# A cross-network tower on one Trainium2 core: product (2, 6) of layer 2 split like its neighbours, its difference on VectorE

## The chip, the cores and the metric

The kernel runs on one core of a Trainium2 chip. The metric is the device time of one execution in microseconds. The engines are TensorE (PE in the profile; its weight loads are PEld), VectorE (DVE), ScalarE (ACT), GpSimd (POOL) and SyncE (SP), whose queue issues most DMAs.

## The reference

The batch has 1024 rows. 32 tables are looked up with `ids`, giving `x0` of 32 fields by 16 embedding elements for each row. Three cross layers follow:

```python
for i in range(n_layers):
    z = (x0[:, :, None, :] * h[:, None, :, :]).reshape(B, F * G, E)
    y = jax.nn.relu(jnp.einsum('oc,bce->boe', Ws[i], z) + bs[i][None, :, None])
    if i != n_layers - 1:
        half = y.shape[1] // 2
        x_keep, h = (y[:, :half, :], y[:, half:, :])
    else:
        x_keep, h = (y, y)
    xs.append(x_keep)
return jnp.sum(jnp.concatenate(xs, axis=1), axis=2)
```

Each layer has 128 outputs; layers 1 and 2 have 32 x 64 = 2048 inputs, the products of a field with a row of the layer before. The sums over the embedding, joined with 16 dense features, go through three dense layers (272 to 512, to 256, to 1). All values are float32.

## The kernel before, in words

The work is cut into 32 tiles of 128 batch rows by 4 embedding elements, 512 columns each; four tiles make a block of 128 rows. An *item* (layer, n) is two chunks of 128 products (128 x 1024 values). VectorE multiplies (L1070), TensorE sums the products with the weights (L617, L625, L640) into one PSUM bank per layer, ScalarE adds the bias, applies the relu and hands `h` to the next layer (`go_on`, L815; `keep`, L821).

There are two kinds of item. A **whole** item is a plain fp32 product: VectorE writes it to one of four `prod` buffers, TensorE takes it with two fp32 matmuls (L617), which the trace shows as four records. A **split** item is written to `unsplit`; ScalarE casts it to fp32r in `high` (L829); `low` = unsplit - high is made by a subtraction whose inputs and output are all in SBUF (`split_low`: L500 on GpSimd, L1078 on VectorE). TensorE then takes four matmuls of `high`, with the high and low parts of the weights (L625), and two of `low` (L640). `kind_of` (L99) says which kind an item is: layers 0 and 1 are whole, layer 2 is split with its difference on GpSimd, except (2, 6), which is whole with weights of its own, `w2T_whole`. In the last slot (2, 2), (2, 5) and (2, 7) have their difference on VectorE.

The order is written out by hand. In steady state all engines go through the same list of 19 steps per tile, a *slot*:

```python
SLOT = [(1, 0), (1, 1), (2, 0), (1, 2), (2, 1), (1, 3), (0, 0), (2, 2), TAIL, (1, 4), (0, 1),
        (2, 3), (1, 5), (2, 4), (1, 6), (2, 5), (1, 7), (2, 6), (2, 7)]
```

Layer 1 belongs to the slot's tile, layer 0 to the tile after, layer 2 to the tile before. TAIL is half an item of layer 0, split between ScalarE (L852, L853) and GpSimd (`tail_parts`, L508). TensorE takes the `low` of a split item one item later (`multiply_low` in `slot`). It transposes the next tile's fields after (2, 4) (`turn_x`, L589), and ScalarE copies them out after (2, 5) (`take_x`, L809). After (2, 4) ScalarE waits for (0, 1) and makes h0 (`next_h0`). After (1, 1) VectorE adds to `acc_kept` (L1101, or L1097 for the first tile of a block).

GpSimd issues the 32 table lookups of the block after next in its slots (L490), eight a slot, placed by `LOOKUPS_FIRST` and `LOOKUPS_AFTER` behind its differences:

```python
LOOKUPS_AFTER = ((0, 0, 2, 0, 1, 2, 3), (0, 0, 1, 1, 1, 2, 2))
LOOKUPS_FIRST = (0, 1)
```

The first row is for *quarter* 0, the second for quarters 1, 2 and 3. A slot has quarter 0 if in it a new block begins for the lookups: after (2, 2) ScalarE waits for the block's 32 lookups to land and copies them to `emb` (`take_rows`, L793), then goes on to TAIL; GpSimd takes the next ids after that (`begin`) and looks up again. Per quarter 0, with layer-2 items 0 to 5 and 7, GpSimd issues two lookups after (2, 2), one after (2, 4), two after (2, 5) and three after (2, 7); in the other quarters one first, one after each of (2, 2), (2, 3), (2, 4), two after (2, 5) and two after (2, 7).

Of the kernel before, what the change touches and what calls it, by code (L numbers as in the profile page):

```python
# [38 lines left out]
P = 128  # L39
# [6 lines left out]
ITEM = 2  # L46
GROUP = 4
CHUNKS = FIELDS * HALF // P
GROUPS = CHUNKS // GROUP
# [36 lines left out]
WHOLE, BY_POOL, BY_DVE = range(3)  # L86
SPLIT = (BY_POOL, BY_DVE)
RING = (4, 4, 2)
WHOLE2 = (2, 6)
LAST_BY_DVE = [(2, 2), (2, 5), (2, 7)]  # L90

ADD_KEPT_AFTER = (1, 1)
# [5 lines left out]

def kind_of(item, last):  # L99

    if item[0] < 2 or item == WHOLE2:
        return WHOLE
    return BY_DVE if last and item in LAST_BY_DVE else BY_POOL

# [18 lines left out]
def of_kind(items, kind, last=False):  # L125
    return [x for x in items if x != TAIL and kind_of(x, last) == kind]


class Plan:
# [13 lines left out]
    def kind(self, s, item):  # L143
        return kind_of(item, self.is_last(s))
# [22 lines left out]
def dlrm_tower(nc, dense_ctx, ids, tables, w_top1, b_top1, w_top2, b_top2, w_top3,  # L167
# [8 lines left out]
    with ExitStack() as ctx:  # L176
        def sb(name, shape, dt=F32):
            return ctx.enter_context(nc.sbuf_tensor(name, shape, dt))
# [20 lines left out]
        w0T = sb("w0T", [P, GROUP, P])  # L199
        w0T_tail = sb("w0T_tail", [P, P], F32R)  # L200
        w1T = sb("w1T", [P, CHUNKS, P])
        w2T_high = sb("w2T_high", [P, CHUNKS, P], F32R)
        w2T_low = sb("w2T_low", [P, CHUNKS, P], F32R)
        w2T_whole = sb("w2T_whole", [P, ITEM, P])
        wt3 = sb("wt3", [P, TOP2 // P])

        dense_parts = sb("dense_parts", [P, batch], F32R)
# [347 lines left out]
        def _(pe):  # L555
# [20 lines left out]
            for b in range(BLOCKS):  # L576
                last = pe.transpose((y0, y1)[b // GROUP][:, P * (b % GROUP):P * (b % GROUP + 1)], dense_wide[:, b, :],
                                    ident[:, :])
# [14 lines left out]
            def accumulator(s, layer):  # L593
                return y2[(s[1] - 1) % 2] if layer == 2 else (y0, y1)[layer]

            def begin_layer(s, layer):

                if layer == 0:
                    pe.wait_ge(s_kept0, number(s) + 1)
                elif layer == 1:  # L600
                    pe.wait_ge(s_kept1, number(s))
                elif not isinstance(s[0], int) or number(s) >= 2:
                    pe.wait_ge(s_sum2, number(s) - 2 + 1)

            def multiply(s, item):

                layer, n = item
                y = accumulator(s, layer)
                if n == 0:
                    begin_layer(s, layer)  # L610
                e, kind = plan.entry(s, item), plan.kind(s, item)
                if kind == WHOLE:
                    z = prod[plan.place(s, item, RING)]
                    pe.wait_ge(s_made[kind], e + 1)
                    for c in range(ITEM):
                        w = w2T_whole[:, c, :] if layer == 2 else (w0T, w1T)[layer][:, ITEM * n + c, :]
                        last = pe.matmul(y[:, :], w, z[:, c, :], start=(n == 0 and c == 0),  # L617
                                         stop=(item in (LAST0, LAST1) and c == ITEM - 1))
                    last.then_inc(s_used[kind], 1)
                else:  # L620
                    z = high[kind][plan.place(s, item, RING)]
                    pe.wait_ge(s_high[kind], e + 1)
                    for c in range(ITEM):
                        for w in (w2T_high, w2T_low):
                            pe.matmul(y[:, :], w[:, ITEM * n + c, :], z[:, c, :],  # L625
                                      start=(n == 0 and c == 0 and w is w2T_high), stop=False)
# [17 lines left out]
            def slot(s, between={}):  # L644
                items = plan.items(s)
                nxt = after(s, 2)
                turn_after = (2, 4) if (2, 4) in items else items[-1]
                waiting = None
                for item in items:
                    if item != TAIL:  # L650
                        multiply(s, item)

                    if waiting:
                        multiply_low(s, waiting)
                    waiting = item if item == TAIL or plan.kind(s, item) != WHOLE else None
                    if item in between:
                        first_unit(between[item])
                    if item == turn_after and (not isinstance(s[0], int) or number(nxt) < TILES):
                        if waiting and item == items[-1]:
                            multiply_low(s, waiting)  # L660
                            waiting = None
                        turn_x(nxt)
                if waiting:
                    multiply_low(s, waiting)
# [4 lines left out]
            for n, c in enumerate(FIRST_ORDER):  # L669
                pe.wait_ge(s_rotated, n + 1)  # L670
                for e in range(QUAD):
                    last = pe.transpose(first_shifted[c][:, P * e:P * (e + 1)], rotated[c][:, P * e:P * (e + 1)], ident[:, :])
# [12 lines left out]
            def top1(unit, col):  # L685

                _, n, m = unit
                rows = slice(TOP1 * n, TOP1 * (n + 1))
                cols = slice(TOP1 * col + P * m, TOP1 * col + P * (m + 1))
                return three_passes(unit_bank[unit][:, :], wt1_high[:, cols], wt1_low[:, cols],  # L690
                                    z_high[n][col][:, :], z_low[col][:, rows], stop=(col == 1))
# [249 lines left out]
        def _(dve):  # L941
# [40 lines left out]
            for n, home in enumerate(homes):  # L982
                dve.wait_ge(s_turned, n + 1)
                source = prep[1][:, 0, :] if n == 1 else prep[n % 2]
                if n == 1:
                    dve.tensor_copy(home, source).then_inc(s_tail_w, 1)

                    dve.wait_ge(s_tail_w, 1)
                    for quarter in (1, 3):
                        lanes = slice(FIELDS * quarter, FIELDS * (quarter + 1))  # L990
                        last = dve.tensor_tensor(w0T_tail[lanes, :], source[lanes, :],
                                                 w0T_tail[lanes, :].bitcast(F32), ALU.subtract)
                    last.then_inc(s_stored, 1)
                elif n in lows:
                    if WHOLE2[1] // (GROUP // ITEM) == n - 2 - GROUPS:
                        of = ITEM * WHOLE2[1] % GROUP
                        dve.tensor_copy(w2T_whole[:, :, :], source[:, of:of + ITEM, :])
                    dve.tensor_copy(home, source).then_inc(s_w_high, 1)

                    dve.wait_ge(s_w_high, sorted(lows).index(n) + 1)  # L1000
                    dve.tensor_tensor(lows[n], source, home.bitcast(F32), ALU.subtract).then_inc(s_stored, 1)
                else:
                    dve.tensor_copy(home, source).then_inc(s_stored, 1)
# [229 lines left out]
```

## Time and profile before

| | |
|---|---|
| median of 3 runs | 1061.19 us (1061.14 to 1063.73) |
| the profiled execution, its own time | 1066.62 us |
| its span | 1064.8 us |
| TensorE busy | 995.8 us (94%) |
| VectorE busy | 821.8 us (77%) |
| ScalarE busy | 474.4 us (45%) |
| GpSimd busy | 816.3 us (77%) |
| mean granted TensorE clock | 0.976 of full speed |

The profile comes from one execution; the span runs from its first to its last instruction. The times in the rows are microseconds from the span's start, with mean durations in nanoseconds in the tables by tile. Busy times count each engine's own instructions. Records of TensorE are pipelined and overlap, so the pace is read from the starts of successive records, not from their durations.

### The profile page before, as it was taken

Reading aid. Unit: us, or ns where it says so; the run is one execution under the profiler, and the core shown is the slowest. Engines: PE = TensorE matmul, PEld = TensorE weight load, DVE = VectorE, ACT = ScalarE, POOL = GpSimd, SP = SyncE. Lnnn points to the kernel's source line nnn. Section 1 sums busy time; section 2 is a strip of 40 time slices with the busy share of each in tenths; the row PEclk is TensorE's granted clock in tenths of the full one; section 3 lists DMA queues with packets and bytes.
Section 4 is the critical chain, followed back from the end, with each engine's and each line's share of the span. In section 5 each row is a group of like instructions: output and inputs, shape, how many; then the busy total and the mean of one; then the engine's idle time right before and its main releaser. Section 6 shows DMA issues by size and latency. Waiting matters only on the chain.

```text
span 1064.8 us, 11324 instructions
## 1 busy us (share of the span) xinstructions
PE 995.8 (94%) x3089; PEld 572.8 (54%) x3089; DVE 821.8 (77%) x750; ACT 474.4 (45%) x595; POOL 816.3 (77%) x524
## 2 busy tenths in 40 slices
PE   3178899999999999999999999999899999999988
PEld 2133455555555555555555555555455555555565
DVE  6234877798778977899778977898778977788882
ACT  2222544444544454454444454444444454543443
POOL 7655779887998879887998789886998766566540
PEclk9579999999999999999999999999999999999989
DMA  8089999989888888899888888888888888889000
GB/s 158 10 189 198 205 199 190 210 191 197 191 194 191 191 192 185 192 198 208 191 194 186 194 188 190 187 192 191 195 187 188 192 186 192 190 186 219 30 1 0
DMA packets 49012, 185.45 MB, mean 174 GB/s; under 512 B 17570, under 2 KB 22178, under 8 KB 28388
## 3 DMA queue, kind: packets, MB, share of 16 engines
q1 hardware_dynamic: 40804, 183.15, 78.2%
q0 software_dynamic: 8192, 2.11, 2.0%
q8 instruction: 7, 0.11, 0.0%
q14 instruction: 9, 0.07, 0.0%
HBM read 182.06 MB, written 3.15 MB: 174 GB/s over the span
## 4 chain that ended last, share of the span: by engine, by line
POOL 42%; PE 26%; issue 18%; DMA 7%; DVE 4%; ACT 2%; SPq 0%; POOLq 0%; ACTq 0%; DVEq 0%
POOL low L500 24%; POOL looked_up L490 16%; PE y L617 15%; PE y L625 6%; DMA looked_up<-in_tbl,ids_now 4%; PE y L640 3%; POOL tail_parts L508 2%; DMA spread<-xcols 2%; DVE unsplit L1070 1%; DVE prod L1070 1%; DMA xcols<-xrows 0%; ACT emb L793 0%; ACT tail_high L853 0%; PE y L721 0%; DVE acc_kept L1101 0%
## 5 line engine op out<-in xcount | busy, mean ns | idle before, releaser
L500 POOL TENSOR_TENSOR low<-unsplit,high 128x1024 fp32r<-128x1024 f32 x221 | 525.1, 2388 | 113.3 <-ACT high L829 111.5
L617 PE MATMUL y<-prod,w1T 128*128 128x512 f32 x1024 | 480.3, 597 | 5.4 <-ACT kept L821 2.7
L1070 DVE TENSOR_TENSOR prod<-spread,h 128x1024 f32<-128x1024 f32 x288 | 349.1, 1216 | 118.3 <-PE y L617 102.6
L829 ACT CAST high<-unsplit 128x1024 fp32r<-128x1024 f32 x224 | 234.0, 1045 | 243.6 <-DVE unsplit L1070 243.2
L1070 DVE TENSOR_TENSOR unsplit<-spread,h 128x1024 f32<-128x1024 f32 x224 | 272.1, 1215 | 48.8 <-ACT h L815 48.6
L490 POOL DMA_INDIRECT looked_up<-in_tbl,ids_now x256 | 248.7, 971 | 69.1 <-issue 59.4
L617 PEld LDWEIGHTS y<-prod,w1T 128*128 128x128 f32 x1024 | 193.5, 192 | 166.8 <-issue 144.1
L625 PE MATMUL y<-high,w2T_high 128*128 128x512 f32 x448 | 226.7, 506 | 4.4 <-ACT high L829 4.4
L640 PE MATMUL y<-low,w2T_high 128*128 128x512 f32 x448 | 202.7, 533 | 6.3 <-POOL low L500 6.3
L625 PE MATMUL y<-high,w2T_low 128*128 128x512 f32 x448 | 177.9, 397 | 0.0
L815 ACT ACTIVATE h<-y,bias 64x512 f32<-64x512 f32 x128 | 83.3, 651 | 209.2 <-PE y L617 208.3
L640 PEld LDWEIGHTS y<-low,w2T_high 128*128 128x128 f32 x448 | 84.4, 191 | 91.3 <-issue 61.5
L617 PE MATMUL y<-prod,w0T 128*128 128x512 f32 x256 | 122.2, 600 | 5.5 <-DVE prod L1070 5.5
L625 PEld LDWEIGHTS y<-high,w2T_high 128*128 128x128 f32 x448 | 84.9, 190 | 50.0 <-issue 29.4
L625 PEld LDWEIGHTS y<-high,w2T_low 128*128 128x128 f32 x448 | 84.9, 190 | 43.4 <-issue 29.0
L1070 DVE TENSOR_TENSOR prod<-shifted,xT 128x1024 f32<-128x1024 f32 x64 | 77.7, 1215 | 22.8 <-DMA shifted<-xcols 15.4
L617 PEld LDWEIGHTS y<-prod,w0T 128*128 128x128 f32 x256 | 48.9, 192 | 49.3 <-issue 45.0
L508 POOL TENSOR_TENSOR tail_parts<-tail,tail_high 128x512 fp32r<-128x512 f32 x32 | 41.0, 1283 | 25.7 <-ACT tail_high L853 25.6
L617 PE MATMUL y<-prod,w2T_whole 128*128 128x512 f32 x128 | 60.1, 592 | 0.0
L821 ACT ACTIVATE kept<-y,bias_kept 64x512 f32<-64x512 f32 x64 | 43.7, 682 | 1.6
L809 ACT COPY xrows<-xT 48x512 f32<-48x512 f32 x32 | 18.5, 579 | 50.6 <-PE xT L589 50.6
L589 PE MATMUL xT<-ident,four_times 128*128 128x128 f32 x128 | 20.2, 282 | 22.2 <-ACT four_times L801 22.2
(115 smaller groups left out, 441.3 us busy)
## 6 DMA issues: line engine op xcount, KB each, us to landing
spread<-xcols SPq DMA_DIRECT2D x128, 1024.0 KB, 9.0
shifted<-xcols SPq DMA_DIRECT2D x124, 256.0 KB
shifted_tail<-xcols SPq DMA_DIRECT2D x124, 64.0 KB
looked_up<-in_tbl,ids_now POOLq DMA_INDIRECT x256
xcols<-xrows SPq DMA_DIRECT2D x32, 96.0 KB, 2.0
spread<-in_L_rec_W SPq DMA_DIRECT2D x3, 512.0 KB, 7.0
spread<-in_L_rec_W SPq DMA_DIRECT2D x1, 1024.0 KB, 11.6
wt<-in_W_top SPq DMA_DIRECT2D x2, 512.0 KB, 8.7
```

What stands on the lines that cost most here:

```text
L490: pool.indirect_dma_start(out=looked_up[:, f, :], out_offset=None, in_=tables[f][:, :], in_offset=bass.IndirectOffsetOnAxis(ap=ids_now[:, ...
L500: pool.tensor_tensor(low[kind][r][:, :, :], unsplit[kind][r][:, :, :], high[kind][r][:, :, :].bitcast(F32), ALU.subtract).then_inc(s_low[k ...
L508: pool.tensor_tensor(tail_parts[:, :], tail[:, :], tail_high[:, :].bitcast(F32), ALU.subtract).then_inc(s_tail_low, 1)
L589: last = pe.transpose(xT[:, P * e:P * (e + 1)], four_times[:, e, :, :].rearrange("p a f -> p (a f)"), ident[:, :])
L617: last = pe.matmul(y[:, :], w, z[:, c, :], start=(n == 0 and c == 0), stop=(item in (LAST0, LAST1) and c == ITEM - 1))
L625: pe.matmul(y[:, :], w[:, ITEM * n + c, :], z[:, c, :], start=(n == 0 and c == 0 and w is w2T_high), stop=False)
L640: last = pe.matmul(accumulator(s, layer)[:, :], w2T_high[:, ITEM * n + c, :], z[:, c, :], start=False, stop=(item == LAST2 and c == ITEM - 1))
L809: act.copy(xrows[:, :], xT[0:XROWS, :]).then_inc(s_xrows, 1)
L815: last = act.activation(h[to, :], y[lanes, :], ACT.Relu, bias=bias[lanes, :])
L821: act.activation(kept[t[1] % KEPT][lanes, :], y[lanes, :], ACT.Relu, bias=bias_kept[lanes, :]).then_inc(s_kept, 1)
L829: act.copy(high[kind][r][:, :, :], unsplit[kind][r][:, :, :]).then_inc(s_high[kind], 1)
L1070: dve.tensor_tensor(z, x[:, ITEM * n:ITEM * (n + 1), :], b[:, :].unsqueeze(1).to_broadcast([P, ITEM, COLS]), ALU.mult).then_inc(s_made[kin ...
```

## The change

Item (2, 6) is split in every slot. Its difference is made by VectorE, behind the product (2, 7), in all slots but the last, where GpSimd makes it. ScalarE casts it between `take_x` and the cast of (2, 7). The plain copy of its weights goes, with the tensor that held it. The two `high` and `unsplit` buffers that VectorE's items had in the last slot serve for it.

```diff
-WHOLE2 = (2, 6)
+SPLIT2_BY_DVE = [(2, 6)]
 LAST_BY_DVE = [(2, 2), (2, 5), (2, 7)]
...
 def kind_of(item, last):
-    if item[0] < 2 or item == WHOLE2:
+    if item[0] < 2:
         return WHOLE
-    return BY_DVE if last and item in LAST_BY_DVE else BY_POOL
+    return BY_DVE if item in (LAST_BY_DVE if last else SPLIT2_BY_DVE) else BY_POOL
...
-        w2T_whole = sb("w2T_whole", [P, ITEM, P])
...
-                        w = w2T_whole[:, c, :] if layer == 2 else (w0T, w1T)[layer][:, ITEM * n + c, :]
+                        w = (w0T, w1T)[layer][:, ITEM * n + c, :]
...
-                    if WHOLE2[1] // (GROUP // ITEM) == n - 2 - GROUPS:
-                        of = ITEM * WHOLE2[1] % GROUP
-                        dve.tensor_copy(w2T_whole[:, :, :], source[:, of:of + ITEM, :])
```

VectorE at the end of a slot, before (`prod<-spread,h_0` is (1, 7), `prod<-spread,h` is (2, 6), the last `unsplit` is (2, 7), `h_1` begins the next slot with (1, 0)):

```order
112 L1070 TENSOR_TENSOR prod<-spread,h_0 128x1024 [waits s_used0]
113 L1067 REGISTER_ALU
114 L1070 TENSOR_TENSOR prod<-spread,h 128x1024 [waits s_used0]
115 L1067 REGISTER_ALU
116 L1070 TENSOR_TENSOR unsplit<-spread,h 128x1024 [waits s_used1]
117 L1067 REGISTER_ALU [waits s_spread10,s_h0]
118 L1070 TENSOR_TENSOR prod<-spread,h_1 128x1024 [waits s_used0]
```

and now (L1074 is the subtraction, four lines up from where it was):

```order
112 L1066 TENSOR_TENSOR prod<-spread,h_0 128x1024 [waits s_used0]
113 L1066 TENSOR_TENSOR unsplit<-spread,h 128x1024 [waits s_used2]
114 L1063 REGISTER_ALU
115 L1066 TENSOR_TENSOR unsplit<-spread,h 128x1024 [waits s_used1]
116 L1074 TENSOR_TENSOR low_54<-unsplit,high 128x1024 [waits s_high2]
117 L1063 REGISTER_ALU [waits s_spread10,s_h0]
118 L1066 TENSOR_TENSOR prod<-spread,h_1 128x1024 [waits s_used0]
```

The subtraction, which waits for ScalarE's cast (`s_high2`), stands in front of the next slot's (1, 0), (1, 1) and acc_kept.

TensorE at the same place, before, from the `low` of (2, 5) on:

```order
210 L640 MATMUL y_1<-low_49,w2T_high 128x512 [waits s_low1]
211 L640 MATMUL y_1<-low_49,w2T_high 128x512
212 L614 REGISTER_ALU
213 L617 MATMUL y_1<-prod,w2T_whole 128x512 [waits s_made0]
214 L617 MATMUL y_1<-prod,w2T_whole 128x512
215 L622 REGISTER_ALU
216 L625 MATMUL y_1<-high,w2T_high 128x512 [waits s_high1]
```

and now, from the four matmuls of (2, 6)'s `high` on:

```order
216 L624 MATMUL y_1<-high,w2T_high 128x512 [waits s_high2]
217 L624 MATMUL y_1<-high,w2T_low 128x512
218 L624 MATMUL y_1<-high,w2T_high 128x512
219 L624 MATMUL y_1<-high,w2T_low 128x512
220 L621 REGISTER_ALU
221 L624 MATMUL y_1<-high,w2T_high 128x512 [waits s_high1]
...
225 L639 MATMUL y_1<-low_54,w2T_high 128x512 [waits s_low2]
226 L639 MATMUL y_1<-low_54,w2T_high 128x512
227 L639 MATMUL y_1<-low_50,w2T_high 128x512 [waits s_low1]
228 L639 MATMUL y_1<-low_50,w2T_high 128x512
```

The two fp32 matmuls have become four before (2, 7) and two after it.

## Rows read from the trace of the kernel before

**Rows 1.** The page, busy us (share of the span) and instructions of each engine.
```profile
PE 995.8 (94%) x3089; PEld 572.8 (54%) x3089; DVE 821.8 (77%) x750; ACT 474.4 (45%) x595; POOL 816.3 (77%) x524
```

**Rows 2.** Windows of four tiles: length, busy us of each engine, clock, DMA.
```profile
core 0: us, PE busy (x) PEld busy (x) DVE busy (x) ACT busy (x) POOL busy (x), PEclk, DMA share, GB/s
394.00:511.00 117.00, 116.99 (x364) 67.00 (x363) 97.62 (x86) 55.41 (x69) 101.76 (x66) 1.00 0.89 193
862.00:979.00 117.00, 117.00 (x365) 67.20 (x364) 96.06 (x86) 54.94 (x68) 71.15 (x33) 1.00 0.87 192
```

**Rows 3.** Timeline of TensorE around (2, 7): start, duration, records merged, idle before.
```profile
508.04 0.40 PE L625 MATMUL y<-high,w2T_high 128*128 128x512 f32 x1
...
508.98 1.88 PE L617 MATMUL y<-prod,w1T 128*128 128x512 f32 x4
...
514.27 3.60 PE L617 MATMUL y<-prod,w1T 128*128 128x512 f32 x8
517.31 0.80 PE L625 MATMUL y<-high,w2T_high 128*128 128x512 f32 x1
517.94 0.39 PE L625 MATMUL y<-high,w2T_low 128*128 128x512 f32 x1
```

**Rows 4.** TensorE's waits for GpSimd's differences (us, times, longest), and one of them.
```profile
PE y L640 <- POOL low L500: 6.3, 8, 1.4
...
520.68 0.30 PEld L640 LDWEIGHTS y<-low,w2T_high 128*128 128x128 f32 x2 [1.00 <-POOL low L500]
...
520.68 0.73 PE L640 MATMUL y<-low,w2T_high 128*128 128x512 f32 x2 [0.17 <-POOL low L500]
```

**Rows 5.** Timeline of ScalarE: casts of (2, 7), the copy of emb; and emb's copies.
```profile
477.30 1.04 ACT L829 CAST high<-unsplit 128x1024 fp32r<-128x1024 f32 x1
...
492.69 0.62 ACT L793 COPY emb<-looked_up 128x512 f32<-128x512 f32 x1 [1.71 <-DMA looked_up<-in_tbl,ids_now]
...
506.62 1.04 ACT L829 CAST high<-unsplit 128x1024 fp32r<-128x1024 f32 x1
...
L793 ACT COPY emb<-looked_up x8: 613/618/622, 47.5 to 849.0; 128x512 f32<-128x512 f32 x8
```

**Rows 6.** Timeline of GpSimd: differences (L500), lookups (L490), tail_parts.
```profile
445.98 2.37 POOL L500 TENSOR_TENSOR low<-unsplit,high 128x1024 fp32r<-128x1024 f32 x1 [1.67 <-ACT high L829]
...
475.30 2.38 POOL L500 TENSOR_TENSOR low<-unsplit,high 128x1024 fp32r<-128x1024 f32 x1 [1.57 <-ACT high L829]
...
483.85 0.94 POOL L490 DMA_INDIRECT looked_up<-in_tbl,ids_now  x1 [0.30 <-issue]
...
495.81 1.29 POOL L508 TENSOR_TENSOR tail_parts<-tail,tail_high 128x512 fp32r<-128x512 f32 x1 [2.35 <-ACT tail_high L853]
...
506.20 2.39 POOL L500 TENSOR_TENSOR low<-unsplit,high 128x1024 fp32r<-128x1024 f32 x1
508.75 0.96 POOL L490 DMA_INDIRECT looked_up<-in_tbl,ids_now  x1 [0.16 <-issue]
...
510.99 2.36 POOL L500 TENSOR_TENSOR low<-unsplit,high 128x1024 fp32r<-128x1024 f32 x1
...
518.24 7.06 POOL L500 TENSOR_TENSOR low<-unsplit,high 128x1024 fp32r<-128x1024 f32 x3
...
744.01 0.96 POOL L490 DMA_INDIRECT looked_up<-in_tbl,ids_now  x1 [3.80 <-issue]
```

**Rows 7.** Timelines of VectorE's adds to acc_kept and GpSimd's work beside them.
```profile
274.06 0.68 DVE L1101 TENSOR_TENSOR acc_kept<-acc_kept,kept 128x512 f32<-128x512 f32 x1
274.28 1.28 POOL L490 DMA_INDIRECT looked_up<-in_tbl,ids_now  x1 [0.30 <-issue]
...
450.27 3.38 DVE L1101 TENSOR_TENSOR acc_kept<-acc_kept,kept 128x512 f32<-128x512 f32 x1
450.73 2.36 POOL L500 TENSOR_TENSOR low<-unsplit,high 128x1024 fp32r<-128x1024 f32 x1
453.26 1.24 POOL L490 DMA_INDIRECT looked_up<-in_tbl,ids_now  x1 [0.16 <-issue]
```

**Rows 8.** The last slot: three of GpSimd's differences and VectorE's (2, 2) beside them.
```profile
1013.55 8.10 POOL L500 TENSOR_TENSOR low<-unsplit,high 128x1024 fp32r<-128x1024 f32 x3 [1.30 <-ACT high L829]
...
1016.37 3.02 DVE L1078 TENSOR_TENSOR low<-unsplit,high 128x1024 fp32r<-128x1024 f32 x1
```

## Prediction, before the result was known

> **What bounds the kernel now.** I read the busy times first, then a whole block of four tiles as windows, then the timeline of TensorE, then its waits. TensorE (PE) is busy 995.8 of 1064.8 us; VectorE (DVE) and GpSimd (POOL) stand at 77% each [rows 1]. In the middle TensorE has no gap: 116.99 of 117.00 us with its clock at 1.00, and 117.00 again in a block near the end [rows 2]. What differs between the two blocks is GpSimd: 101.76 us busy in the first, where it issues 32 table lookups beside its differences, 71.15 in the second, where there are no lookups left. So I expect the plain answer "TensorE work saved is time saved" in the late tiles, and have to look closer at the blocks with lookups.
>
> There the waits show one weak place. TensorE waited for a GpSimd difference (L500) 8 times, 6.3 us in all [rows 4]. At 520.68 its weight load (PEld) had stood idle 1.00 us for low(2,0) of a quarter 1, and TensorE itself 0.17. Blocks with lookups show next to no other gap [rows 2], so TensorE arrives there about when the difference does, or a little earlier. I follow that difference back. GpSimd works without a pause from 495.81 (tail_parts) to low(2,0), which starts at 518.24 [rows 6]. 495.81 is released by tail_high on ScalarE (ACT), this by the copy of emb at 492.69, which waited 1.71 us for the last lookup to land [rows 5]. That lookup was issued at 483.85, at the end of the GpSimd stretch that began at 475.30, which itself waited 1.57 us for ScalarE's cast, and this in the program for TensorE's (0,1), whose result ScalarE handles before it. So **one chain per block** runs from TensorE's quarter 3 through GpSimd, a DMA and GpSimd again to TensorE's quarter 1, over 45 us long (475.30 to 520.6), and TensorE does two (2,6) products beside it. In quarters 1 and 2 GpSimd catches up (at 445.98, in quarter 2, it waits 1.67 us), so that half is TensorE's own.
>
> **The change part by part.**
> TensorE: four records of a whole product go, six split ones come. Eight whole records from 514.27 and one split one to 517.94 take 3.67 us, the four split ones from 508.04 to 508.98 0.94, the one from 517.31 on, which starts while the whole ones still drain, is followed by steps of 0.23 in the whole timeline; I take 0.233 [rows 3]. A whole record is (3.67 - 0.23) / 8 = 0.43. The item falls from 4 x 0.43 = 1.72 to 6 x 0.233 = 1.40: 0.32 us, 32 times, 10.3 us if nothing else bound.
>
> ScalarE: one more cast of 1.04 us a slot. It goes in front of the cast of (2,7), which starts at 506.62 and for which GpSimd comes at 510.99 at the earliest; it is hidden, but it fixes when VectorE can begin: 507.7 in quarter 0 and 478.4 in quarter 3 [rows 5].
>
> VectorE: one more subtraction of 128x1024 per slot, 1.12 us when alone (it ran until 1.12 us after GpSimd's op at 1016.37) [rows 8]. Behind it queue the next slot's (1,0) and (1,1), now made at 509.7 and 510.8 in quarter 0, where TensorE starts them at 514.27: hidden. Then comes acc_kept, and then (2,0), due at 517.3. The ring of plain products loses one item in eleven, which only loosens it. The copy of w2T_whole in the preparation goes; the first lookups, until 47.5 us, cover it: nothing.
>
> GpSimd: no work more, but the meeting with VectorE is the price. What the rows show: an add of VectorE with both inputs in SBUF that took 0.68 us at 274.06 took 3.38 at 450.27, until 0.56 us after GpSimd's difference of 450.73 had ended; and the lookups that followed such an add took 1.24 and 1.28 us where 0.94 to 0.97 is usual [rows 7]. A difference behind one of VectorE's was late too: 8.10 us for three at 1013.55 [rows 8], 7.06 at 518.24 [rows 6]. So the two exclude each other both ways, lookups included. A lookup that finds the port taken ends 0.85 us after VectorE (453.26 + 1.24 against 453.65).
> The Trainium skill (SBUF — State Buffer, Who interferes with whom) says that a VectorE instruction with two SBUF inputs and a GpSimd one that reads SBUF block each other; the trace agrees, with 3.38 us. It holds, as inferred, that descriptor generation is not held up by a tensor_tensor; the lookups of 1.24 and 1.28 us speak against it. By that sentence this part would cost nothing, the first rival below.
>
> For the chain this gives, per block:
> - quarter 3: VectorE's new difference runs 478.4 to 479.5, across the start of the second lookup at 479.08; that ends at 479.52 + 0.85 = 480.37 instead of 480.02: **+0.35**. Bounds 0 (it fits between) and 0.8 (below).
> - quarter 0: it is ready at 507.7 while GpSimd's low(2,5) runs from 506.20 to 508.57, takes the port then until 509.69, and the lookup of 508.75 ends at 510.54 instead of 509.71: **+0.83**. Bounds 0 and 1.12.
> - quarter 0 again: acc_kept, made ahead of low(2,7) until now, comes at 511.9, behind low(2,7), and holds the lookup after it as at 453.26: **+0.28**. Bounds 0 and 0.5.
> Sum +1.46 us a block. A block whose chain binds gains nothing from the two (2,6) items beside it. Emb is copied 8 times [rows 5]; the first belongs to the start and the last has no lookups behind it, so 6 chains. The other 32 - 12 = 20 items give their 0.32. Quarters 1 and 2 suffer similar holds (up to 0.6 us), but GpSimd waits 1.67 us at 445.98 [rows 6], so they stay hidden.
> Sum: 6 x 1.46 - 20 x 0.32 = 8.8 - 6.4 = +2.4, less 0.3 as the first chain has such a held lookup already: **+2.1 us**. The last slot, where (2,6) goes to GpSimd, I put at nothing (bounds -0.3, TensorE's gain, which is already counted, and +1.6, if the new difference makes VectorE wait just before (2,7)).
> The profiled execution took 1066.62 (span 1064.8); it holds one pause of 3.80 us on GpSimd's lookups at 744.01 [rows 6] that the median of the runs, 1061.19, need not have. The sum is made on the former and carried over: 1061.2 + 2.1 = **1063.3 us**.
>
> **The rivals.**
> 1. *The gain stays* (chance 0.22). Lookups are not held by VectorE, or its op slips into the 0.3 us gaps and less is held than I count. Then the chain has its old length: -20 x 0.32 = -6.4, 1054.8 us. For it: the lookups stand 0.3 us apart (483.85), and an add that begins there runs in 0.68 us (274.06). Against: the 1.24 and 1.28 us of the lookups behind such adds. With a chain that does not bind at all it would be -10.3, 1050.9; [rows 4] speak against.
> 2. *VectorE loses the port in quarters 2 and 3* (0.12). At 450.27 its add began 0.46 us ahead of GpSimd's difference and still lost. If the new difference, begun 0.6 us into a lookup, loses in the same way, it runs only after low(2,7), one tile before the one of [rows 6] and so at 482.4, until 483.5. (1,0), (1,1), acc_kept and (2,0) follow with 1.13 + 1.13 + 0.3 + 1.2, its cast with 1.1: 488.4. TensorE wants it at 517.31 - 29.32 (a tile, 477.30 to 506.62 in [rows 5]) - 0.32 = 487.7. That is 0.7 us a tile in 12 tiles, 8.4, and 0.45 more on each chain, 2.7: about 1074. If only quarter 3 is hit, 1070. The point from which it decides is the start of VectorE's difference against the next GpSimd op: it must win with 0.7 us ahead.
> The terms of the forecast at their bounds, 6 x (0 to 2.4) - 6.4, give -6.4 to +8.
>
> **How the numbers follow.** My forecast has 0.66, rival 1 0.22, rival 2 0.12. A measurement can tell about 0.3%, 3.2 us. Within the forecast the chain's terms may be off by a third, 6 x (1.0 to 2.0) - 6.7, which gives -0.7 to +5.3 beside its own range of 1060 to 1067, so a bit over a third of it lies above 1064.4. Faster: 0.22 (rival 1 and none of the forecast). Same: 0.44. Slower: 0.12 + 0.22 = 0.34. The range takes in rival 1 at 1054.8 and the lower half of rival 2: 1054 to 1069.
>
> **What would show it.** Right: TensorE's item (2,6) at 1.40 us; in a block with lookups the new wait of TensorE at low(2,7) of quarter 0 and at low(2,0) of quarter 1, together near 2 us; the copies of emb 0.8 us further apart; one lookup of about 1.8 us per block behind low(2,5) of quarter 0; tiles after 866 us at 29.0 instead of 29.32. Wrong: lookups all at 0.95 (rival 1), VectorE differences of over 3 us in quarters 2 and 3 with TensorE waiting for ScalarE's cast (rival 2), or TensorE waiting for products (1,0), (1,1) in every tile.

## The result, and the profile after

Over 20 runs of each kernel on the same chip, the changed kernel took **1065.25 us** (median; 1062.5 to 1067.5) and the kernel before 1062.99 us (1060.33 to 1065.91). The ratio is **1.0021, 95% interval 1.0012 to 1.003**: 2.3 us slower. A second set, on another chip (experiment 9 below), gave 1.0017. The forecast was 2.1 us slower, which counted as "Same" there. TensorE does less work and the kernel does not become faster.

The two profiled executions must not be subtracted from each other. The one of after is the shortest of its runs (1062.5 us, span 1060.7), the one of before is longer than any of those 20 (1066.62, span 1064.8). What can be compared is the distance between like events.

The page of the changed kernel, against [rows 1]: busy time and instructions of each engine, and of the costly groups three (busy us, mean ns of one | idle before).

```profile
PE 985.6 (93%) x3153; PEld 585.1 (55%) x3153; DVE 848.0 (80%) x780; ACT 505.1 (48%) x627; POOL 832.3 (78%) x525
...
L499 POOL TENSOR_TENSOR low<-unsplit,high 128x1024 fp32r<-128x1024 f32 x222 | 529.6, 2399 | 100.9 <-ACT high L828 98.6
...
L489 POOL DMA_INDIRECT looked_up<-in_tbl,ids_now x256 | 260.1, 1016 | 68.7 <-issue 59.6
...
L1074 DVE TENSOR_TENSOR low<-unsplit,high 128x1024 fp32r<-128x1024 f32 x34 | 50.1, 1472 | 117.5 <-ACT high L828 117.5
```

TensorE is busy 10.2 us less, the amount forecast. GpSimd is busy 16.0 us more with one instruction more; most of it lies in its 256 lookups (L489), which it issues as before. They took 248.7 us before and take 260.1 now, 1016 ns instead of 971 each. VectorE's differences (L1074) average 1472 ns; alone one takes 1.21.

Windows of four tiles, the stretches of [rows 2]: length, PE busy (x) PEld DVE ACT POOL, clock, DMA share, GB/s.

```profile
394.00:511.00 117.00, 115.68 (x370) 68.15 (x368) 100.53 (x90) 59.72 (x73) 103.37 (x65) 1.00 0.89 192
862.00:979.00 117.00, 117.00 (x375) 69.71 (x375) 99.24 (x92) 58.37 (x71) 73.52 (x33) 1.00 0.89 198
```

In the late block TensorE still has no gap, and VectorE's new differences start 29.02 us apart (then at 919.98 and 949.00), where a tile took 29.32 before:

```profile
861.94 1.22 DVE L1074 TENSOR_TENSOR low<-unsplit,high 128x1024 fp32r<-128x1024 f32 x1 [4.57 <-ACT high L828]
890.96 1.23 DVE L1074 TENSOR_TENSOR low<-unsplit,high 128x1024 fp32r<-128x1024 f32 x1 [4.58 <-ACT high L828]
```

In the block with lookups TensorE now has 1.3 us of gaps, at two places (the window ends inside the second). Between 150 and 1000 us it waits 10.1 us for GpSimd's differences, 11 times; before it was 5.0 us, 7 times. Its timeline around them (start, duration, records merged, idle before and who ended it), against [rows 3, 4]:

```profile
509.77 0.63 PE L639 MATMUL y<-low,w2T_high 128*128 128x512 f32 x2
511.51 0.73 PE L639 MATMUL y<-low,w2T_high 128*128 128x512 f32 x2 [1.11 <-POOL low L499]
512.08 3.60 PE L616 MATMUL y<-prod,w1T 128*128 128x512 f32 x8
...
519.04 0.73 PE L639 MATMUL y<-low,w2T_high 128*128 128x512 f32 x2 [0.72 <-POOL low L499]
```

The first wait is for low(2,7) of quarter 0, the second for low(2,0) of quarter 1, 1.83 us together (the record at 509.77 is low(2,6), VectorE's new difference, which is there in time). GpSimd and VectorE at the same place, where [rows 6] have a lookup of 0.96 us behind low(2,5):

```profile
503.46 2.42 POOL L499 TENSOR_TENSOR low<-unsplit,high 128x1024 fp32r<-128x1024 f32 x1
506.04 1.77 POOL L489 DMA_INDIRECT looked_up<-in_tbl,ids_now  x1 [0.16 <-issue]
508.11 0.95 POOL L489 DMA_INDIRECT looked_up<-in_tbl,ids_now  x1 [0.30 <-issue]
509.08 2.38 POOL L499 TENSOR_TENSOR low<-unsplit,high 128x1024 fp32r<-128x1024 f32 x1
511.62 1.24 POOL L489 DMA_INDIRECT looked_up<-in_tbl,ids_now  x1 [0.16 <-issue]
```

```profile
504.43 2.54 DVE L1074 TENSOR_TENSOR low<-unsplit,high 128x1024 fp32r<-128x1024 f32 x1 [4.58 <-ACT high L828]
506.89 2.34 DVE L1066 TENSOR_TENSOR prod<-spread,h 128x1024 f32<-128x1024 f32 x2
509.15 2.86 DVE L1097 TENSOR_TENSOR acc_kept<-acc_kept,kept 128x512 f32<-128x512 f32 x1
```

VectorE's difference is ready at 504.43 while GpSimd's low(2,5) runs, and ends at 506.97, 1.1 us after it. The lookup that meets it ends at 507.81, 0.84 us after VectorE's end: 1.77 us instead of 0.96. acc_kept, ready beside low(2,7), does the same to the lookup behind that: 1.24 instead of 0.97. In quarter 3 the same pair looks like this (GpSimd, then VectorE):

```profile
472.35 2.38 POOL L499 TENSOR_TENSOR low<-unsplit,high 128x1024 fp32r<-128x1024 f32 x1 [0.97 <-ACT high L828]
474.87 0.96 POOL L489 DMA_INDIRECT looked_up<-in_tbl,ids_now  x1
476.14 1.32 POOL L489 DMA_INDIRECT looked_up<-in_tbl,ids_now  x1 [0.30 <-issue]
```

```profile
475.42 1.23 DVE L1074 TENSOR_TENSOR low<-unsplit,high 128x1024 fp32r<-128x1024 f32 x1 [2.69 <-ACT high L828]
```

Here VectorE's difference starts inside a lookup and keeps its 1.23 us; only the second lookup is held, to 1.32 us. So per block the lookups and differences of the chain grow by 0.38, 0.81 and 0.27 us: 1.46 us, the sum of the prediction, term by term. These are the blocks in the middle; not every block has all three holds (see the step "So 6 chains" below).

What becomes of it shows in ScalarE's copies of emb, one a block, against [rows 5]:

```profile
371.56 0.62 ACT L792 COPY emb<-looked_up 128x512 f32<-128x512 f32 x1 [1.76 <-DMA looked_up<-in_tbl,ids_now]
489.96 0.62 ACT L792 COPY emb<-looked_up 128x512 f32<-128x512 f32 x1 [1.93 <-DMA looked_up<-in_tbl,ids_now]
```

From the second of the eight on they are at 137.22, 253.85, 371.56, 489.96, 608.29, 726.44 and 847.36. Before they were at 139.83, 256.99, 374.99, 492.69, 610.26, 727.85 and 849.02. The three middle blocks (fourth copy to seventh) took 117.57 to 117.70 us before and take 118.15 to 118.40 now.

### The profile page after: what moved, and what is told of

Its sections match the earlier page's. It is cut to its first block, busy times and chain, and to the rows that moved or that the text cites. A ratio compares the mean times of both kernels' runs of the same rounds, so it can differ in the third digit from the quotient of the medians.

```text
span 1060.7 us, 11459 instructions
## 1 busy us (share of the span) xinstructions
PE 985.6 (93%) x3153; PEld 585.1 (55%) x3153; DVE 848.0 (80%) x780; ACT 505.1 (48%) x627; POOL 832.3 (78%) x525
## 4 chain that ended last, share of the span: by engine, by line
POOL 38%; PE 31%; issue 16%; DMA 6%; DVE 6%; ACT 3%; SPq 0%; POOLq 0%; DVEq 0%; ACTq 0%
POOL low L499 21%; PE y L616 17%; POOL looked_up L489 15%; PE y L624 7%; PE y L639 4%; DMA looked_up<-in_tbl,ids_now 3%; DVE unsplit L1066 2%; DMA spread<-xcols 2%; DVE prod L1066 2%; POOL tail_parts L507 1%; DMA xcols<-xrows 0%; PE xT L588 0%; ACT emb L792 0%; ACT high L828 0%; DVE z_kept_low L1143 0%
## 5 line engine op out<-in xcount | busy, mean ns | idle before, releaser
L828 ACT CAST high<-unsplit 128x1024 fp32r<-128x1024 f32 x256 | 264.6, 1045 | 253.5 <-DVE unsplit L1066 252.9
L1066 DVE TENSOR_TENSOR prod<-spread,h 128x1024 f32<-128x1024 f32 x256 | 307.1, 1211 | 18.6 <-ACT h L814 9.0
L489 POOL DMA_INDIRECT looked_up<-in_tbl,ids_now x256 | 260.1, 1016 | 68.7 <-issue 59.6
L1066 DVE TENSOR_TENSOR unsplit<-spread,h 128x1024 f32<-128x1024 f32 x256 | 307.3, 1210 | 4.6 <-ACT h L814 4.6
L624 PE MATMUL y<-high,w2T_high 128*128 128x512 f32 x512 | 239.4, 468 | 4.9 <-ACT high L828 4.9
L639 PE MATMUL y<-low,w2T_high 128*128 128x512 f32 x512 | 219.4, 517 | 12.6 <-POOL low L499 12.6
L624 PE MATMUL y<-high,w2T_low 128*128 128x512 f32 x512 | 203.2, 397 | 0.0
L639 PEld LDWEIGHTS y<-low,w2T_high 128*128 128x128 f32 x512 | 96.4, 191 | 101.1 <-issue 64.5
L1074 DVE TENSOR_TENSOR low<-unsplit,high 128x1024 fp32r<-128x1024 f32 x34 | 50.1, 1472 | 117.5 <-ACT high L828 117.5
L624 PEld LDWEIGHTS y<-high,w2T_high 128*128 128x128 f32 x512 | 96.8, 189 | 47.7 <-issue 19.1
L624 PEld LDWEIGHTS y<-high,w2T_low 128*128 128x128 f32 x512 | 96.7, 189 | 40.0 <-issue 21.5
## 6 DMA issues: line engine op xcount, KB each, us to landing
wt<-in_W_top SPq DMA_DIRECT2D x2, 512.0 KB, 10.1
```

What stands on the lines that cost most here:

```text
L489: pool.indirect_dma_start(out=looked_up[:, f, :], out_offset=None, in_=tables[f][:, :], in_offset=bass.IndirectOffsetOnAxis(ap=ids_now[:, ...
L624: pe.matmul(y[:, :], w[:, ITEM * n + c, :], z[:, c, :], start=(n == 0 and c == 0 and w is w2T_high), stop=False)
L639: last = pe.matmul(accumulator(s, layer)[:, :], w2T_high[:, ITEM * n + c, :], z[:, c, :], start=False, stop=(item == LAST2 and c == ITEM - 1))
L828: act.copy(high[kind][r][:, :, :], unsplit[kind][r][:, :, :]).then_inc(s_high[kind], 1)
L1066: dve.tensor_tensor(z, x[:, ITEM * n:ITEM * (n + 1), :], b[:, :].unsqueeze(1).to_broadcast([P, ITEM, COLS]), ALU.mult).then_inc(s_made[kin ...
L1074: dve.tensor_tensor(low[kind][r][:, :, :], unsplit[kind][r][:, :, :], high[kind][r][:, :, :].bitcast(F32), ALU.subtract).then_inc(s_low[ki ...
```

## The experiments

The theory (A) is the one of the prediction: the cost comes from VectorE's two SBUF inputs, which hold GpSimd's lookups, on a chain that binds in the blocks with lookups. Rivals: the added VectorE work itself or ScalarE's cast costs it whatever the operands are (B), and TensorE bounds the blocks, so the saving is lost elsewhere.

**1. One input from PSUM.** The difference of (2, 6) is as long and as wide, but its second input is a PSUM tile; its values are not the difference.

```diff
+if item == (2, 6):
+    dve.tensor_tensor(low[kind][r][:, :, :], unsplit[kind][r][:, :, :],
+                      h0[s[1] % 2][:, :].unsqueeze(1).to_broadcast([P, ITEM, COLS]), ALU.subtract)
```

> The changed kernel, but VectorE's new difference takes its second input from PSUM (the bank of h0 that stands there) instead of high in SBUF; same size, same waits, same place, so the result of (2, 6) is not the layer's. Port theory (VectorE's op with two SBUF inputs and GpSimd's ops lock each other out, and each lock lengthens the chain of lookups): the locks of the difference go, only acc_kept stays behind low(2,7) at 0.28 us a block. 6 x 0.28 - 20 x 0.32 = -4.7 us against the kernel before, about 1058.3, ratio 0.9956; lookups behind low(2,5) of quarter 0 back at 0.96 us. Rival (VectorE's queue: the op's time and its wait for the cast hold up the products behind it, whatever its inputs): as the changed kernel, ratio 1.002.

Measured: 1059.2 us (1057.39 to 1061.19), ratio to before 0.996 (0.9946 to 0.9974). Lookups and VectorE at quarter 0:

```profile
502.70 2.41 POOL L499 TENSOR_TENSOR low<-unsplit,high 128x1024 fp32r<-128x1024 f32 x1
505.27 0.96 POOL L489 DMA_INDIRECT looked_up<-in_tbl,ids_now  x1 [0.16 <-issue]
...
510.07 1.24 POOL L489 DMA_INDIRECT looked_up<-in_tbl,ids_now  x1 [0.16 <-issue]
```

```profile
504.13 1.22 DVE L1075 TENSOR_TENSOR low<-unsplit,h 128x1024 fp32r<-128x1024 f32 x1 [4.57 <-ACT high L828]
```

The operation now runs straight through GpSimd's difference in 1.22 us, and the lookup behind it takes 0.96. Six us of the changed kernel's time hang on where one operand lies, with every instruction kept. B falls. The PSUM input here is also one that is read twice over, where `high` is read once. The changed kernel itself speaks against this as the cause: VectorE's adds to `acc_last` take a plain 128x512 input from PSUM, and a lookup that starts 0.14 us behind one takes its usual time:

```profile
463.11 0.73 DVE L1110 SCALAR_TENSOR_TENSOR acc_last<-y,neg_last,acc_last 128x512 f32<-128x512 f32 x1
463.25 0.97 POOL L489 DMA_INDIRECT looked_up<-in_tbl,ids_now  x1 [0.16 <-issue]
```

The acc_kept hold of 1.24 us stays, since that add still has both inputs in SBUF.

**2 and 3. The kernel before, with the operation alone.** The old kernel gets one unused subtraction of 128x1024 a slot where the change puts its difference, once with both inputs in SBUF, once with one from PSUM. TensorE's work is unchanged.

```diff
+if item == (2, 7) and not plan.is_last(s):
+    dve.wait_ge(s_high[BY_POOL], plan.entry(s, item) + 1)
+...
+    dve.tensor_tensor(unsplit[BY_DVE][0][:, :, :]..., w1T[:, 0:2 * GROUP, :],
+                      w1T[:, 2 * GROUP:4 * GROUP, :], ALU.subtract).then_inc(s_spare, 1)
```

> The kernel before plus one subtraction of 128x1024 on VectorE with two SBUF inputs (two halves of w1T, output unused), behind the product (2,7), after ScalarE's cast of (2,7), which is when the cast of (2,6) ends in the changed kernel. Nothing on TensorE. Port theory: each of six chains longer by 1.46 us, less 0.3 once: +8.5 us, ratio 1.0080. Rival (queue): whatever it costs here it costs in the next run too.

> The same addition to the kernel before, with one input in PSUM. Port theory: only acc_kept's shift behind low(2,7) costs, 6 x 0.28 = +1.7 us, ratio 1.0016. Rival (queue): equal to the run with two SBUF inputs.

Measured: two SBUF inputs 1069.98 us, ratio 1.0057 (1.0044 to 1.0071); one from PSUM 1063.86, ratio 1.0008 (0.9999 to 1.0017). So the operation costs nearly nothing and its operands 6.1 us. Here the profiled executions lie within 0.2 us of their medians, and the distances of emb between the second copy and the last, which should carry it, give it back: 853.26 - 137.34 = 715.92 against 847.05 - 137.52 = 709.53, 6.4 us. Quarter 0 shows the same collision as after:

```profile
507.33 2.37 POOL L501 TENSOR_TENSOR low<-unsplit,high 128x1024 fp32r<-128x1024 f32 x1
509.86 1.77 POOL L491 DMA_INDIRECT looked_up<-in_tbl,ids_now  x1 [0.16 <-issue]
```

In experiment 3 the subtraction runs across the start of the same lookup and does not hold it:

```profile
505.44 1.22 DVE L1175 TENSOR_TENSOR unsplit<-w1T,h 128x1024 f32<-128x1024 f32 x1 [3.76 <-ACT high L830]
```

```profile
506.45 0.96 POOL L491 DMA_INDIRECT looked_up<-in_tbl,ids_now  x1 [0.16 <-issue]
```

It keeps the acc_kept hold (a lookup of 1.24 us at 511.21), so by the terms the two differ by 1.18 us a block. From one copy of emb to the issue of the next block's last lookup the way is 110.27 us in 2 (493.86 to 604.13) and 109.10 in 3 (490.43 to 599.53): 1.17. Against the kernel before (108.89, 492.69 to 601.58) it is 1.38 of the expected 1.46, but a part is lost in the landing: from that issue to the copy it took 8.34 to 8.61 us in 2 and 8.68 to 8.84 before. Experiment 1 has 8.48 to 8.67 with no hold in quarter 3, so it is not the hold that shortens it. It moves by up to 0.5 us from kernel to kernel, and is part of why 1.0057 was measured and not 1.0080. Another part is the last block: in quarter 0 of it no lookup of 1.77 us stands, and it is 0.5 us longer than before (121.68 against 121.17), not 1.46.

**4. One input from PSUM in quarter 0 only** (the edit of experiment 1 with `and (s[1] + 2) % TILES_PER_BLOCK == 0`).

> The changed kernel with the PSUM input in slots of quarter 0 alone; in the others the real difference. The result of (2, 6) is wrong in those slots. Port theory: 0.83 us a block goes, 0.35 of quarter 3 and 0.28 of acc_kept stay: 6 x 0.63 - 6.4 - 0.3 = -2.9 us, ratio 0.997. Rival (queue): 1.002.

Measured: 1061.87 us, ratio 0.9985 (0.9975 to 0.9994). The 1.77 us lookups are gone, those of quarter 3 stay:

```profile
476.43 1.33 POOL L489 DMA_INDIRECT looked_up<-in_tbl,ids_now  x1 [0.30 <-issue]
...
506.28 0.96 POOL L489 DMA_INDIRECT looked_up<-in_tbl,ids_now  x1 [0.16 <-issue]
```

Quarter 0's term is worth 1065.25 - 1061.87 = 3.4 us and the others' 1061.87 - 1059.2 = 2.7 (the first of the three medians is from another set of runs on a chip where the kernel before took the same, 1062.99 and 1063.09). By the prediction's terms it would have been 0.83 : 0.35, but each total is only known to 1 or 1.5 us. The blocks in the middle tell the terms apart better: 118.29 and 118.38 us on average in the two profiles of the changed kernel, 117.56 here and 117.23 in experiment 1, so 0.73 to 0.82 us for quarter 0 and 0.33 for quarter 3.

**5 and 6. No lookups in the steady part.** Both kernels keep only the first block's lookups and use its rows for all blocks. GpSimd's differences and VectorE's stay.

```diff
-pool.wait_ge(s_looked, 16 * FIELDS * b)
+pool.wait_ge(s_looked, 16 * FIELDS)
...
+if not looking[0]:
+    return
```

> The kernel before without the table lookups of blocks 1 to 7 (all blocks use block 0's embeddings, so the output is block 0's arithmetic repeated). Chain theory: TensorE loses nothing at low(2,0) of quarter 1 any more, 6 x 0.35 us plus what the start loses: about -3 us, ratio 0.997. If the lookups bound nothing: 1.000.

> The changed kernel without those lookups. Chain theory: all 32 items give their 0.32 us, so 10.3 us under the run of the kernel before without lookups: about 1050, ratio 0.9875, although VectorE and GpSimd still meet at the port in every slot. Rival (VectorE's op and the port cost time everywhere, chain or not): less than half of it, ratio above 0.992.

Measured: 1060.23 us for the kernel before and 1050.31 for the changed one, ratios 0.993 (0.9917 to 0.9942) and 0.9838 (0.9823 to 0.9854) to the full kernel before, which took 1067.57 on this chip. The difference between the two is 9.9 us: **TensorE's whole saving of 10.2 us comes out once the chain is gone.** The window of the changed kernel without lookups:

```profile
394.00:511.00 117.00, 117.00 (x376) 69.29 (x376) 97.08 (x92) 59.88 (x74) 72.95 (x35) 1.00 0.87 193
```

TensorE has no gap, and the copies of emb are 116.06 apart (368.48, 484.54); in the kernel before without lookups they are 117.25 apart. The first number was expected nearer to 1 (0.997). From the second copy of emb to the last the kernel before takes 7.6 us less without lookups (701.62 against 709.19). The middle blocks give the 0.3 to 0.4 us that were expected, down to TensorE's own 117.25. What was missed is 3.9 us in the block with the 3.80 us pause of [rows 6], which goes with the lookups, and 1.3 and 1.2 us in the first two blocks.

With that the blocks of all these kernels can be set against the terms (us between copies of emb from the fourth to the seventh, so without the first chains and without the pause):

| kernel | TensorE | holds | two (2, 6) beside the chain | by the terms | measured |
|---|---|---|---|---|---|
| before | whole | 0 | 0 | (117.65) | 117.57 to 117.70 |
| after, and again (exp. 9) | split | 1.46 | -0.64 | 118.5 | 118.15 to 118.47 |
| 1, PSUM | split | 0.28 | -0.64 | 117.3 | 117.18 to 117.27 |
| 4, PSUM in quarter 0 | split | 0.63 | -0.64 | 117.6 | 117.54 to 117.58 |
| 2, before + two SBUF | whole | 1.46 | 0 | 119.1 | 118.72 to 118.89 |
| 3, before + PSUM | whole | 0.28 | 0 | 117.9 | 117.61 to 117.95 |
| 5, before, no lookups | whole | no chain | | | 117.25 |
| 6, after, no lookups | split | no chain | | | 116.06 |

The terms are added to 117.65, the middle of the kernel before. The "-0.64" is worth a look. The chain passes through TensorE (from a quarter 1 to the next quarter 3), so the two cheaper items there shorten it, even where it binds; experiments 1 and 4 show this.

**7 and 8. Lookups moved out of the chain.** The hope was a version that keeps the saving. In quarters 1 to 3 the lookup at the head of the slot and one of those behind (2, 7) go; one more comes behind (2, 2) and one behind (2, 4).

```diff
-LOOKUPS_AFTER = ((0, 0, 2, 0, 1, 2, 3), (0, 0, 1, 1, 1, 2, 2))
-LOOKUPS_FIRST = (0, 1)
+LOOKUPS_AFTER = ((0, 0, 2, 0, 1, 2, 3), (0, 0, 2, 1, 2, 2, 1))
+LOOKUPS_FIRST = (0, 0)
```

> The kernel before with the lookups of quarters 1 to 3 placed earlier or later: none first, two after (2,2), one after (2,3), two after (2,4), two after (2,5), one after (2,7), so that one fewer stands between low(2,5) of quarter 3 and the block's last lookup and none before low(2,0) of quarter 1. Chain theory: the chain is shorter by up to 2.5 us a block and no longer binds; the kernel before gains the 0.35 us a block it lost, about -2 us, ratio 0.998.

> The changed kernel with the same placing of the lookups. Chain theory: its chain binds by about 2.2 us a block (118.35 against 4 x 29.0), the placing takes up to 2.5 off, so most of the 10.3 us appears: 1052 to 1056, ratio 0.990 to 0.993, faster than both kernels. Rival (the cost is not in the chain): 1.000 to 1.002.

Measured: the kernel before with this order 1071.76 us, ratio 1.0038 (1.0024 to 1.0051). The changed one 1103.79, ratio **1.0338 (1.0322 to 1.0354)**. Both expectations missed, the second by over 40 us. Waits of TensorE between 150 and 1000 us of the second (us, times, longest), GpSimd and VectorE in a quarter that is not 0, and a wait of TensorE one slot on:

```profile
PE y L639 <- POOL low L499: 36.4, 25, 3.9
```

```profile
439.69 2.40 POOL L499 TENSOR_TENSOR low<-unsplit,high 128x1024 fp32r<-128x1024 f32 x1
442.24 1.77 POOL L489 DMA_INDIRECT looked_up<-in_tbl,ids_now  x1 [0.16 <-issue]
```

```profile
440.09 3.08 DVE L1074 TENSOR_TENSOR low<-unsplit,high 128x1024 fp32r<-128x1024 f32 x1 [3.46 <-issue]
...
445.36 2.85 DVE L1097 TENSOR_TENSOR acc_kept<-acc_kept,kept 128x512 f32<-128x512 f32 x1
```

```profile
478.48 0.74 PE L639 MATMUL y<-low,w2T_high 128*128 128x512 f32 x2 [1.49 <-POOL low L499]
```

The extra lookup behind (2, 4) lets low(2,5) start later. In the changed kernel VectorE's difference of quarter 3 begins at 475.42, only 0.69 us after low(2,5) has ended (474.73). Here low(2,5) still runs at 440.09 when the difference is ready, so the collision of quarter 0 happens in **every** slot: 1.77 us lookups at 411.29, 442.24, 473.02 and 503.81. Each slot then starts late and the next collides too. Blocks are 122.4 to 123.0 us apart, but for one of 129.4 that holds the pause described below. The same order of lookups costs the kernel before only 4.2 us, so it takes the order and VectorE's difference together.

**9. The changed kernel again**, beside 10 to 12 on one chip.

> The changed kernel once more, beside the next three on the same chip: ratio 1.002.

Measured: 1069.85 us, before 1067.85 on this chip, ratio 1.0017 (1.0006 to 1.0029), as expected. Its profiled execution lies 0.6 us from the median. Copies of emb at 142.96, 259.87, 378.28, 496.75, 614.99, 733.43 and 855.28.

**10 to 12. Two smaller moves.** The lookup behind (2, 4) of quarter 0 goes behind (2, 7) (10); in addition the first lookup of quarters 1 to 3 goes behind (2, 2) (11); 12 is the order of 11 in the kernel before.

```diff
-LOOKUPS_AFTER = ((0, 0, 2, 0, 1, 2, 3), (0, 0, 1, 1, 1, 2, 2))
+LOOKUPS_AFTER = ((0, 0, 2, 0, 0, 2, 4), (0, 0, 1, 1, 1, 2, 2))
```

> The changed kernel; in quarter 0 the lookup after (2,4) goes behind (2,7) (none after (2,4), four after (2,7)), nothing else. GpSimd's low(2,5) then ends about 1.2 us earlier, before ScalarE's cast of (2,6), so VectorE's difference finds the port free. Port theory: no lookup of 1.77 us in quarter 0, low(2,7) 2 us earlier and TensorE's wait there (1.0 to 1.1 us a block) gone, low(2,0) of quarter 1 0.83 us earlier: 5 to 6 x 0.8 = 4 to 5 us under the changed kernel, ratio 0.998 against the kernel before. Rival (only the number of lookups ahead of low(2,0) counts, which stays): 1.002.

> As the run before, and in quarters 1 to 3 the lookup that stood first goes behind (2,2) (two there, none first), so low(2,0) of quarter 1 comes another 1.25 us earlier; nothing moves between low(2,3) and (2,7), which the other moved order had changed. Chain theory: the chain is 2.1 us shorter a block and hardly binds, nearly all of the 10.3 us appears: 1053 to 1056 on a chip where the kernel before has 1063, ratio 0.990 to 0.993. If low(2,1) or the landing of the lookups binds next: 0.995 to 0.997.

> The kernel before with the same order of lookups as the run before. Chain theory: only the 0.35 us a block that it loses at low(2,0) of quarter 1 can come back, 1 to 2 us, ratio 0.998 to 0.999; so the split of (2,6) is worth 6 to 9 us between these two.

Measured: 1071.51, 1086.62 and 1070.47 us; ratios 1.0041 (1.0024 to 1.0058), 1.0181 (1.0167 to 1.0195) and 1.002 (1.001 to 1.003). All three missed. In 10 the three differences run on without a break, and VectorE's begins just as they end; it still holds the lookup (not in every block: at 393.72, where VectorE starts 0.01 us ahead, it takes 0.96 us, and that block is 117.48 us long where the next two are 118.62 and 118.23):

```profile
504.00 7.02 POOL L499 TENSOR_TENSOR low<-unsplit,high 128x1024 fp32r<-128x1024 f32 x3
511.18 1.90 POOL L489 DMA_INDIRECT looked_up<-in_tbl,ids_now  x1 [0.16 <-issue]
```

```profile
511.01 1.22 DVE L1074 TENSOR_TENSOR low<-unsplit,high 128x1024 fp32r<-128x1024 f32 x1 [4.57 <-ACT high L828]
```

Why the whole of 10 took 1.7 us more than the changed kernel did is not shown; its profiled execution is 3.1 us shorter than its median.

In 11 the lookup that stood first in a slot had filled GpSimd's wait for the cast of (2, 0). Without it GpSimd is idle there, all that follows is later by about 1 us, and the collision of experiment 8 is in every quarter again: 1.77 us lookups at 406.30 (quarter 0), 437.16, 466.68 and 496.21. In 12 the blocks do fall to 117.2 to 117.4 us, TensorE's own pace, so the chain no longer sets the pace there. The time still goes up. One reason lies outside the theory, a pause of GpSimd's lookups. Here it is, in 12:

```profile
331.73 0.95 POOL L490 DMA_INDIRECT looked_up<-in_tbl,ids_now  x1 [8.63 <-issue]
```

It is 3.80 us at 744.01 in the kernel before [rows 6], 3.60 at 742.40 after, 3.47 to 3.80 between 739 and 750 in experiments 1 to 4 and 9, which keep the order of the lookups. It is 7.95, 7.17, 7.16 and 8.63 us between 331 and 339 in 7, 8, 11 and 12, which give up the lookup at the head of the slots, and over 1 us nowhere in 10 and in the two without lookups. So it belongs to the program, not to one execution, and where it is long it takes back what the freed chain gives: in 7 one block took 124.0 us (260.08 to 384.10), before 118.0, and from the second copy of emb to the last 7 took 709.46 us and 12 took 708.97, the kernel before 709.19. That is a gain lost, not yet the 4.2 and 2.6 us by which 7 and 12 are slower. From the first copy of emb to the second they took 91.75 and 92.08 us, where experiments 1 to 4 and 9 took 89.84 to 90.71 (and the long execution of before 92.33); why is open. What the pause waits for, no view shows either.

No order tried here beats both kernels.

## Why the prediction was right, and where it was off

- **The total.** +2.1 us was forecast, +2.3 measured (interval 1.3 to 3.2). The forecast's mechanism and its sign hold; how near the total came is partly luck, as the next points show.
- **TensorE's item at 1.40 us.** Right: busy time fell by 10.2 us, the late tiles by 0.30 us each, and the pair of kernels without lookups differs by 9.9.
- **The three holds.** +0.35, +0.83 and +0.28 were forecast, 0.38, 0.81 and 0.27 measured. That such a lookup ends 0.85 us after VectorE held at 0.84 in the case above and at 0.85 in experiment 10 (511.01 + 1.22 + 0.85 = 511.18 + 1.90). That the two SBUF inputs are the cause is shown by experiments 1 to 3.
- **The new waits** at low(2,7) and low(2,0), "together near 2 us": 1.83. The lookup "of about 1.8 us": 1.77, though not in every block (next point but one).
- **The copies of emb "0.8 us further apart"**: 0.56 to 0.85 in the middle blocks of the two profiles of the changed kernel, +0.82 by the terms.
- **"So 6 chains."** This step failed. The first of the six did not bind in either profile of the changed kernel: the copy of emb at its end (253.85, and 259.87 in experiment 9) did not wait for a lookup, where the one of the kernel before did, and the block took 116.63 and 116.91 us, 117.16 before.

```profile
253.85 0.62 ACT L792 COPY emb<-looked_up 128x512 f32<-128x512 f32 x1
```

```profile
256.99 0.62 ACT L793 COPY emb<-looked_up 128x512 f32<-128x512 f32 x1 [0.87 <-DMA looked_up<-in_tbl,ids_now]
```

The others bound, but not all with the +0.83 of quarter 0. In the second of one profile VectorE's difference came 0.25 us after the lookup had started, and did not hold it:

```profile
269.86 0.96 POOL L489 DMA_INDIRECT looked_up<-in_tbl,ids_now  x1 [0.16 <-issue]
```

```profile
270.11 1.22 DVE L1074 TENSOR_TENSOR low<-unsplit,high 128x1024 fp32r<-128x1024 f32 x1 [4.57 <-ACT high L828]
```

In the last of both profiles the difference ran during the pause of the lookups (741.18 to 742.41, with the lookup at 742.40). These blocks took 117.71 us against 118.00, and 120.92 against 121.17; the last of experiment 9, whose difference ran in the pause too, took 121.85, which this does not explain. From the second copy of emb to the last the two profiles took 710.14 and 712.32 us, before 709.19. That is +1.0 and +3.1 where my terms gave 6 x 0.82 - 0.3 = +4.6.
- **The rest.** Behind the last emb the changed kernel gained 2.4 us in both profiles (213.3 us left of the span, 215.8 before), my 8 x 0.32 = 2.6. With it the distances give -1.5 and +0.7 us. Between these and the measured +2.3 there are 1.6 to 3.8 us that I cannot place in a profile. The profile of before was an unusually long execution, but its middle blocks agree with those of experiment 3; 1.6 to 2.5 us of its excess lie ahead of the second copy (92.33 us from the first, where the changed kernel and experiments 1 to 4 and 9 took 89.84 to 90.71), which the distances above leave out. That part stays open, so that the total came out within 0.2 us is in part luck.
- **The pause.** I wrote that the median "need not have it". It is there in every profile with this order, on both sides of the change, so carrying the sum over to the median was sound. But it took one of the six quarter-0 holds away (above). Reading it as a chance event misled me in experiment 5 and hid the danger in 7 and 12.
- **Rival 1** (the gain stays) falls for this change: the lookups are held. With one operand in PSUM 3.9 us of gain showed against its 6.4, and without lookups the whole. The Trainium skill infers (SBUF — State Buffer, Who interferes with whom) that a tensor_tensor does not hold up descriptor generation; the lookup of 1.77 us instead of 0.96 speaks against it, and the trace decides. What part of a lookup is held, the reading of its ids in SBUF or the rest, no run here separates.
- **Rival 2** (VectorE loses the port in quarters 2 and 3) falls as placed. A difference that begins inside a lookup, 0.4 us before its end and 0.7 us ahead of the next one, wins: 1.23 us in quarters 1 to 3, no wait of TensorE for ScalarE's cast. But a slow loop of its kind exists. It is decided by another point: whether low(2,5) has ended when the cast of (2, 6) has. The change passes by 0.69 us, experiments 8 and 11 don't and took some 34 and 17 us more than the changed kernel did (for 8 the changed kernel's time on that chip is taken as 1.002 x 1067.57, for 11 it is experiment 9's).
- **The last slot at nothing**: right within what can be told (2.4 us behind the last emb against 2.6 for the items alone).

## What to carry to other kernels

Before moving work from the busiest engine to one with spare time, look at what the other engines do at that moment, not at their busy share: here 0.32 us saved on TensorE was paid with 0.4 to 0.8 us on GpSimd's lookups. Find out which chain sets each block and whether it passes through the engine that you relieve. If a two-input VectorE operation meets GpSimd, it was worth 6 us here to have one input in PSUM. And where engines work in a repeating slot, measure the margin in time by which they miss each other: 0.69 us was all that stood between 0.2% and 3.4%.

## What the runs showed of the hardware that I had not expected

- A GpSimd lookup is held by VectorE's two-SBUF-input operation even if both begin within 0.2 us of each other with VectorE ahead: 1.90 us instead of 0.95 (experiment 10), and 2.01 us in experiment 9, where the lookup starts at 275.87 and VectorE at 275.82. It was not held where VectorE began 0.01 us ahead (0.96 us at 393.72, experiment 10) or 0.25 us behind (0.96 us at 269.86, changed kernel). With one input in PSUM no lookup was held (0.96 and 0.97 us, experiments 1 and 3 and the adds to `acc_last`).
- A stream of lookups holds one long pause of 3.5 to 8.6 us at a place fixed by their order in the program, and none of over 1 us in one order.
- The time from the issue of a block's last lookup to the copy that waits for it, 8.0 to 8.9 us in the profiles, moves by up to 0.5 us between blocks in the middle of one kernel and the next, with no hold near it.
